# Gated cross-attention and grouped experts: another order at the ends of the attention stage, and the probabilities' part of the late rows' logits behind the four values

## The reference

```python
# attention: 4 heads of 128, one key/value head, 64 context tokens
x = x + tanh(g_xattn) * xattn(layernorm(x), ctx, mask, rms_scale, q_w, kv_w, out_w)
#   q = rope(rmsnorm(.) @ q_w) * 128**-0.5 ; k = rope(rmsnorm(ctx) @ k_w) ; v = rmsnorm(ctx) @ v_w
#   probs = softmax(where(mask, q @ k, fill)) ; result = (probs @ v) @ out_w
# experts: 128 (32 experts x 4 sets), each picks one of 32 tokens in each group of 32
x = x + tanh(g_ffn) * ffn(layernorm(x), Wc, bc, W1, b1, W2, b2)
#   logits = grouped @ Wc + bc + tie ; perm = (logits == max over the 32 tokens)
#   inner = relu(permuted @ W1 + b1) ; result = perm^T (inner @ W2 + b2)
```

## Time and profile before

| | |
|---|---|
| median of 3 runs | 1724.45 us |
| profiled execution, its own time | 1724.45 us |
| its span, first to last instruction | 1722.6 us, so 1.85 us lie around it |
| mean granted TensorE clock | 0.982 of full speed |
| PE busy | 1594.7 us, 93% of the span |
| DVE, POOL, ACT busy | 1304.8, 862.0, 719.0 us |
| one attention unit | 24.42 us |
| attention ends, first gather of the experts | 862.59 us |

### The profile page before, as it was taken

How to read it: one execution, slowest core, us unless ns; L and a number is a source line. 1 busy time by engine, 2 the same in 40 slices (tenths; PEclk the granted TensorE clock), 3 DMA queues, 4 the chain that set the end, 5 groups by cost and what they waited for, 6 DMA issues and landing times.

```text
span 1722.6 us, 51583 instructions
## 1 busy us (share of the span) xinstructions
PE 1594.7 (93%) x22424; PEld 1140.7 (66%) x22424; DVE 1304.8 (76%) x1893; ACT 719.0 (42%) x966; POOL 862.0 (50%) x1020
## 2 busy tenths in 40 slices
PE   8899999999999999999889888899889988899895
PEld 4678777877777777877666655466655566555662
DVE  5878777887778777877748777777777777777776
ACT  3622323233323322232145455555455554555453
POOL 3477887887778877877621223213123122232213
PEclk9999999999999999999899999999999999999998
DMA  7624545554455545545575788787788777887776
GB/s 292 177 102 153 182 139 183 171 160 156 158 194 164 162 148 189 165 147 171 182 251 161 194 213 219 219 225 213 189 215 218 215 203 201 207 226 219 210 194 170
DMA packets 182705, 325.31 MB, mean 189 GB/s; under 512 B 23120, under 2 KB 35280, under 8 KB 181072
## 3 DMA queue, kind: packets, MB, share of 16 engines
q1 hardware_dynamic: 137216, 239.15, 43.3%
q0 software_dynamic: 17616, 32.52, 11.5%
q10 hardware_dynamic: 27648, 50.34, 9.0%
HBM read 243.23 MB, written 78.71 MB: 187 GB/s over the span
## 4 chain that ended last, share of the span: by engine, by line
PE 72%; DMA 13%; issue 5%; DVE 5%; POOL 3%; ACT 2%; ACTq 1%; SPq 0%; DVEq 0%; POOLq 0%
PE ps L958 19%; PE ps L1493 14%; PE ps L1003 10%; PE ps L1463 7%; DMA gat<-in_W 5%; PE ps L1016 5%; DMA xin<-out 4%; PE ps L971 3%; PE ps L1031 3%; DMA out<-xin 3%; PE ps L1532 2%; PE ps L1517 2%; PE ps L990 2%; PE ps L983 2%; DVE res L1389 1%
## 5 line engine op out<-in xcount | busy, mean ns | idle before, releaser
L184 POOL TENSOR_SCALAR xin<-xin,r_all,nb_all 128x512 f32<-128x512 f32 x128 | 117.1, 917 | 541.6 <-DMA xin<-out 390.8
L1389 DVE STREAM_TRANSPOSE res<-res 128x2048 f32<-128x2048 f32 x128 | 292.1, 2295 | 0.1
L1343 ACT ACTIVATE gat<-ps 128x1536 f32<-128x1536 f32 (+1 forms) x128 | 171.5, 1344 | 229.9 <-PE ps L1463 229.8
L1407 DVE COPY res<-ps 128x1024 f32<-128x1024 f32 x128 | 156.6, 1224 | 62.1 <-PE ps L1517 62.0
L958 PE MATMUL ps<-xTh,qh 128*128 128x512 f32 x512 | 202.6, 396 | 0.9 <-POOL xTl L560 0.8
L958 PE MATMUL ps<-xTh,ql 128*128 128x512 f32 x512 | 199.5, 390 | 0.0
L958 PE MATMUL ps<-xTl,qh 128*128 128x512 f32 x512 | 199.3, 389 | 0.0
L1463 PE MATMUL ps<-sel,xin 32*128 32x128 f32 x4096 | 160.7, 295 | 38.0 <-POOL xin L184 12.9
L1395 DVE COPY gat<-ps 128x512 f32<-128x512 f32 (+1 forms) x128 | 103.9, 815 | 98.2 <-PE ps L1463 97.9
L1463 PEld LDWEIGHTS ps<-sel,xin 32*128 32x128 f32 x4096 | 137.9, 199 | 56.8 <-issue 31.9
L560 POOL TENSOR_TENSOR xTl<-xT,xTh 128x512 fp32r<-128x512 f32 x128 | 161.8, 1297 | 27.2 <-ACT xTh L624 27.2
(11 more groups left out here) (174 smaller groups left out, 3283.9 us busy)
## 6 DMA issues: line engine op xcount, KB each, us to landing
gat<-in_W ACTq DMA_DIRECT2D x192, 256.0 KB, 6.3
xT<-in_xT SPq DMA_DIRECT2D x32, 1024.0 KB, 6.9
xin<-in_x SPq DMA_DIRECT2D x64, 512.0 KB, 3.8
out<-xin SPq DMA_DIRECT2D x64, 512.0 KB, 3.1
xin<-out SPq DMA_DIRECT2D x128, 256.0 KB, 4.4
xin<-in_W SPq DMA_DIRECT2D x128, 256.0 KB, 4.2
out<-xin POOLq DMA_DIRECT2D x120, 256.0 KB, 7.9
xT<-in_W SPq DMA_DIRECT2D x68, 256.0 KB, 4.6
```

Of the source, the lines that this page charges most:

```text
L184: e.tensor_scalar(self.xn[:, t, :], self.xn[:, t, :], self.r[:, i, t:t + 1], self.nb[:, i, t:t + 1], ALU.mult, ALU.add).then_inc(self.m_xn ...
L1343: e.activation(o, v, ACT.Copy).then_inc(m_gaA.sem, 1)
L1389: e.transpose(v, v).then_inc(m_tr.sem, 1)
L1407: e.tensor_copy(o, v).then_inc(m_evV.sem, 1)
```

## The change

- TensorE: for g up to 29, `part_of_values(g)` comes after the four `values(g, t)` and no longer waits for `m_pl`; `values(g, 0)` waits for both parts of `m_pl` and for `m_vl`, the other three for `m_rs` alone. Unit 30 keeps `part_of_values` ahead, and its four values come behind `logits_T(31)`, in loop 31. After the loop come `values(31, 0 to 2)`, the first `chosen_T`, `values(31, 3)`, the second `chosen_T`.
- DVE: `both_parts(g-1)` stands in loop g behind the sums, ahead of `turned(g+1, 0)`. The adds of unit 30 are spread over loop 31 between maxima and sums; its statistics follow `probs_lo(31)`. The picks of batch 0 come between the adds of unit 31, whose statistics all come last. In loop -1 `bias_last(2)` stands behind `turned(0, 3)` instead of ahead of it.
- POOL: in loop -1, the low parts of x of unit 1 come ahead of the low part of the values (L602). Four of batch 0's eight `normed` move from loop 31 to loop 30, ahead of `scaled_logits(28)`.
- ACT: `logits(0)` also waits for `bias_last(2)`. In experts batch 0, the four DMA issues of W2's piece 7 come behind the first two copies of `rest`.
- SP: at u = 30 the two loads of the router's logits come ahead of the unit's outputs.

```diff
@@ sync
+                if u == NU - 2:
+                    for n in range(2):
+                        e.wait_ge(d_lgs[n].sem, d_lgs[n].at((NU - 5 - n) // LX_RING))
+                    e.wait_ge(m_L.sem, m_L.at(NU - 1))
+                    for n in range(2):
+                        route.load_logits(e, 0, n)
                 k = u % RING
...
-                    if h and u == NU - 2:
-                        (the same six lines)
@@ gpsimd
                 if g == NU - 1:
-                    for t in range(NT):
+                    for t in range(TH, NT):
                         route.normed(e, 0, t)
...
+                if g == -1:
+                    for c in range(C):
+                        lo(1, c)
                 if g % 2 and 0 <= b < B:
                     e.wait_ge(m_vh.sem, m_vh.at(b))
                     e.tensor_tensor(vw[:, b % 2, 1], ...)
-                if unit(g + 2):
+                if unit(g) and unit(g + 2):
                     for c in range(C):
                         lo(g + 2, c)
+                if unit(g + 2):
                     norm_scale(g + 2)
...
                     row_scale(g - 1)
+                if g == NU - 2:
+                    for t in range(TH):
+                        route.normed(e, 0, t)
@@ scalar, logits(u)
                     e.wait_ge(d_ksc.sem, d_ksc.at(0, 1))
+                    e.wait_ge(m_b2s.sem, m_b2s.at(0, 2))
@@ vector
                 if unit(g):
                     top_of(g, 0)
                     top_of(g, 1)
+                if g == NU - 1:
+                    add(g - 1, 0)
                 if unit(g):
                     sums(g, 0)
+                if g == NU - 1:
+                    add(g - 1, 1)
+                if unit(g):
                     sums(g, 1)
+                if g == NU - 1:
+                    add(g - 1, 2)
+                    add(g - 1, 3)
+                if unit(g - 1) and g < NU - 1:
+                    both_parts(g - 1)
...
-                if g == -1:
-                    bias_last(2)
-                if unit(g - 1):
+                if unit(g - 1) and g < NU - 1:
                     stats_of_x1(g - 1, 2)
                     stats_of_x1(g - 1, 3)
                 if unit(g + 1):
                     turned(g + 1, 3)
+                if g == -1:
+                    bias_last(2)
...
+                if g == NU - 1:
+                    for t in range(TH):
+                        stats_of_x1(g - 1, t)
+                    moments_of_x1(g - 1)
...
-                if g == NU - 1:
-                    for step in range(3):
-                        route.pick(e, 0, 0, step)
-                if unit(g):
+                if g == NU - 2:
                     both_parts(g)
-                if g == NU - 1:
-                    for step in range(3):
-                        route.pick(e, 0, 1, step)
-                if unit(g):
+                if unit(g) and g < NU - 2:
                     for t in range(2):
                         add(g, t)
                         stats_of_x1(g, t)
                     add(g, 2)
                     add(g, 3)
+            u = NU - 1
+            add(u, 0)
+            (pick of half 0)
+            add(u, 1)
+            (pick of half 1)
+            both_parts(u)
+            add(u, 2)
+            add(u, 3)
+            for t in range(TH):
+                stats_of_x1(u, t)
+            moments_of_x1(u)
@@ tensor, values(u, t)
-                e.wait_ge(m_pl.sem, m_pl.at(u, t // 2))
-                e.wait_ge(m_vl.sem, m_vl.at(u // 2))
+                if t == 0:
+                    for tp in range(2):
+                        e.wait_ge(m_pl.sem, m_pl.at(u, tp))
+                    e.wait_ge(m_vl.sem, m_vl.at(u // 2))
@@ tensor, part_of_values(u)
-                for tp in range(2):
-                    e.wait_ge(m_pl.sem, m_pl.at(u, tp))
+                if u >= NU - 2:
+                    (the same two waits)
@@ tensor, the loop
+                if g == NU - 1:
+                    for t in range(TH):
+                        values(g - 1, t)
                 if unit(g):
                     probs_T(g, 0)
                     probs_T(g, 1)
                 if unit(g + 1):
                     logits(g + 1)
-                if unit(g):
+                if g >= NU - 2:
                     part_of_values(g)
-                    values(g, 0)
-                    values(g, 1)
-                (chosen_T of half 0 at g == NU - 1, then values 2 and 3)
+                elif unit(g):
+                    for t in range(TH):
+                        values(g, t)
+                    part_of_values(g)
+            for t in range(TH - 1):
+                values(NU - 1, t)
+            e.wait_ge(m_pl.sem, m_pl.at(NU - 1, 0))
+            route.chosen_T(e, 0, 0)
+            values(NU - 1, TH - 1)
@@ experts, scalar
-                    if live(i) and t < QUARTERS:
+                    if 0 < i and live(i) and t < QUARTERS:
                         load_second(e, i, W2_MOVED[2], t)
...
                     if live(i):
                         rest(i, u)
+                    if i == 0 and u == 1:
+                        for c in range(QUARTERS):
+                            load_second(e, 0, W2_MOVED[2], c)
```

More of the change, by code:

```diff
@@ L936, in vector @@
                     add(g, 3)
-            stats_of_x1(NU - 1, 2)
-            stats_of_x1(NU - 1, 3)
-            moments_of_x1(NU - 1)
+            u = NU - 1
+            add(u, 0)
+            for step in range(3):
+                route.pick(e, 0, 0, step)
+            add(u, 1)
+            for step in range(3):
+                route.pick(e, 0, 1, step)
+            both_parts(u)
[4 more added lines that the diff above has]
+            moments_of_x1(u)
         def tensor(e):
@@ L1109, in tensor @@
                     logits(g + 1)
-                if unit(g):
+                if g >= NU - 2:
                     part_of_values(g)
-                    values(g, 0)
-                    values(g, 1)
-                if g == NU - 1:
-                    e.wait_ge(m_pl.sem, m_pl.at(g, 0))
-                    route.chosen_T(e, 0, 0)
-                if unit(g):
-                    values(g, 2)
-                    values(g, 3)
+                elif unit(g):
[7 more added lines that the diff above has]
+            values(NU - 1, TH - 1)
             e.wait_ge(m_pl.sem, m_pl.at(NU - 1, 1))
```

## The result

The changed kernel takes 1740.45 us, the median of 6 runs (1735.43 to 1744.8), against 1722.83 us of the kernel before (6 runs). The ratio is 1.0107, with a 95% interval of 1.008 to 1.0134: slower by 14 to 23 us. The forecast was 1747.6 us, slower, in a range of 1738 to 1758. The profiled execution took 1744.8 us, with a span of 1743.0. TensorE's busy time is almost the same (1594.7 before, 1598.7 after), 4 of the 20.4 us by which the two spans differ, so most of the time went into idle stretches.

The account below looks back on a forecast made before the run. The prediction took TensorE, busy for the whole 24.42 us of an attention unit, to bound the kernel. Terms 28.8 + 0.6 - 2.2 - 3.1 - 0.9 = +23.2 us on 1724.45 gave 1747.6 us, range 1738 to 1758.

Parts of the forecast that it names:

- Step 1: Units 0 to 29: moved `part_of_values` delays ACT's `voh`, then `lt`, idling TensorE 1.92 us 15 times; +28.8 us.
- the restart's 0.08 us: At each idle ahead of `logits_T`: 0.08 us added for a first matmul whose weights were not loaded in advance.
- Step 2: Values of units 0 to 29: fewer waits -0.06, later add +0.08, sum +0.02 a unit; +0.6 us.
- The rival of late adds: Every unit also idles 0.3 us at `values(g, 2)` and `values(g, 3)`: +9 instead of +0.6, 1756 us; chance 0.10.
- Step 3: Start of attention: earlier rotation leaves 0.1 us before `vo`-held `lt` is late; earlier `lo(1)` gives most; -2.2 us.
- Step 4: End of attention: unit 30's values fill the 4.51 us idle, but DVE's gather copy is next late; -3.1 us.
- the wait for the two choices: End of attention: TensorE waits once for each half's choice, about 0.8 us each.
- The loss named behind it: DVE has four statistics, 0.64 us each, instead of two ahead of its first gather copy: 861.1 instead of 864.16.
- the step's lower bound: End of attention: -7 us, if weights landing earlier remove waits in batch 0.
- the step's upper bound: End of attention: 0 us, if an idle stretch lowers the clock again.
- Step 5: Experts batch 0: ACT's four W2 piece 7 issues move behind its first copy, so TensorE's third piece comes earlier; -0.9 us.
- The clock rival: The clock falls at each of the fifteen new idle times in attention: +60, 1808 us; chance 0.04.

Follow-up runs that it names:

- experiment 1: Changed kernel with ACT's logits copy `lt` moved ahead of its copy `voh`; 1714.37 us (12 runs), ratio 0.9939 to the kernel before.
- experiment 2: Changed kernel with `part_of_values` back ahead of the values for units 0 to 29, its `m_pl` waits restored; 1713.33 us (12 runs), ratio 0.9941.
- experiment 3: Kernel before with only `part_of_values` moved behind the values (units 0 to 29) and `both_parts` a loop later; 1748.07 us (4 runs), ratio 1.0147.
- experiment 4: Changed kernel with ACT's copy `voh` split into four copies of 64 columns; 1752.4 us in one run.
- experiment 5: Changed kernel with `lt` ahead of `voh`, plus the old `m_pl` and `m_vl` waits back at every values; 1719.16 us in one run.
- experiment 8: Changed kernel with `lt` ahead of `voh`, plus SP's ring load of W1's piece 1 ahead of `scales_back(29)`; 1711.63 us in one run.
- experiment 9: Changed kernel with `lt` ahead of `voh`, plus loop -1 of DVE and POOL as before the change; 1721.2 us in one run.
- experiment 10: Kernel before with only ACT's `lt` moved ahead of `voh`; 1721.76 us in one run.

## Why the prediction was right

**Step 1** (+28.8 us, 15 idle times of 1.92). Right in place, count and size: 2.06 us from the last matmul for 2.07, and a pair of units 1.87 us longer, which makes 28.0 for 15, and +28.6 between `logits_T(1)` and `logits_T(30)` in the traces. Experiments 1 and 2 remove it from either side, 3 makes it alone, 4 moves it with `voh`'s length. What the Trainium skill says of ScalarE's order ("TensorE: Matmul & The Clock Gate", "Architectural detail: the array is 16x 32x32, not 1x 128x128") is borne out by 1 and 4. Of the restart's 0.08 us, 0.06 shows: in a stalled loop the transposes take 0.85 to the queries instead of 0.79.

**Step 2** (+0.6 us). The sum was near, but by luck: both terms were nothing, and they had opposite signs. Waits that are met cost nothing (experiment 5), and the add in time costs nothing: in experiment 1 a unit is 24.42 us as before, without a wait at values in units 0 to 29. The rival of late adds falls.

**Step 3** (-2.2 us). -2.05, by the two mechanisms named: -0.05 to `logits_T(0)`, where the `vo` transfer was next late, and -2.00 from there to `logits_T(1)` by `lo`.

**Step 4** (-3.1 us). The chain came as worked out: with `logits_T(30)` of both traces laid on each other, `pr` comes at 842.25 for 842.3 and `part_of_values(31)` at 846.9 for 847.1. (Only one add lies ahead of `pr`, as the sum has it; with the two that the text names it would be 843.0.) The term that was too large is the wait for the two choices, 0.18 and 0.53 us for 0.8 each, so the first gather came 5.3 us earlier for 4.4. The loss named behind it was the right one: TensorE waited 2.0 us for DVE's copy behind the four statistics, and at the third gather 4.1 us are left for the 3.1 forecast. What follows was not in the forecast: in the profiled execution batch 0 took 3.2 us more, so about 2 of the 5.3 us were left at batch 1. Two things are seen there. The middle weights, whose earlier coming was the step's lower bound, came later against the first gather, 6.3 us behind it for 3.5 (4.1 with the ring load issued earlier); that this makes batch 0 longer is not shown (experiment 8). And what the step's upper bound feared, an idle stretch that lowers the clock again, happened in six of nine profiles with this end. In experiment 1 it was some 3 us at half the clock, which is about 1.6 us lost, where the two profiles of that kernel differ by 1.9 in batch 0. What made batch 0 of the profiled execution longer, where the clock stayed up for 30 us, stays open.

**Step 5** (-0.9 us). The wait that it removes was measured (1.44 us), a gain behind it was not.

**The sum.** +23.2 was forecast, +17.6 measured, and the move alone measured +26.8 for 29.4 (steps 1 and 2). Where the forecast's terms lie, from the end of the preamble to the gather of batch 1, the two traces differ by +24.5. The rest of the change gave -8.0 (experiment 2, ratio 0.9941, interval 0.9908 to 0.9975, so -4 to -16) where -6.2 was forecast, and the traces find only some -4 of it in attention and batch 0. What else it brought in the experts stays open: that stage varies by 10 us between profiles, and the before profile has the longest of them all (812.1 us behind batch 1's gather). So the distance of the whole, 5.6 us, measures no term of the forecast.

**The clock rival** did not come true: 15 idle times of 1.66 us, one in 51 us, left the clock at 1.00 in the changed kernel and in experiment 3. The swing between two levels that the Trainium skill describes ("TensorE: Matmul & The Clock Gate", "A second HAM failure mode: psum-queue depth-cycling") did not show at these idle times. But it was nearer than the 0.04 says: with idle times only 0.28 us longer, experiment 4, the clock fell once in 15. And the evidence I set against it was weaker than I took it: the idle of 2.36 us at the start left the clock alone in the profiles of before and of experiment 3, and lowered it in those of experiments 9 and 10.

## What to carry to other kernels

Before a producer is moved later, list every engine that waits for its signal, and for each what is queued behind that wait: a waiting copy that nobody needs yet is free, until something needed at once stands behind it in the same queue. Such an idle time can be worked out to a few hundredths of a us from rows of the old trace alone. Here the cure was in the waiting queue as well as in the moved work (experiments 1 and 2): one swap of two ACT copies turned +1% into -0.6%.

## What the runs showed of the hardware that I had not expected

- Whether an idle time of 1.9 to 2.4 us lowers TensorE's clock is not settled by its length. 2.36 us at the start left it at 1.00 twice and lowered it to 0.50 twice, at a cost of about 0.5 us in experiment 9 (33.3 against 32.8 us). 1.94 us in experiment 4 lowered it once in 14 times; 2.0 us ahead of the third gather, six times in nine. The 30 of 1.66 us in the changed kernel and experiment 3 never did.
- Six met waits a unit between pipelined matmuls cost TensorE nothing (24.40 us a unit with them, 24.42 without).
- DVE's `bias_last(2)` took 2.36 us when it started together with POOL's L574, the first row below. After the change it took 1.28, and POOL's L573, which now starts 0.16 behind it, 2.24 instead of 1.27: it looks as if one of the two waited for the other.

```profile
74.81 1.29 POOL L574 TENSOR_TENSOR qc<-qc,qs 128x512 f32<-128x512 f32 x1
```
```profile
77.95 1.28 DVE L890 SCALAR_TENSOR_TENSOR b2s<-b2s,part,lt 128x1024 bf16<-128x1024 bf16 x1
```
```profile
78.11 2.24 POOL L573 TENSOR_TENSOR qc<-qc,qs 128x512 f32<-128x512 f32 x1
```
